# A graph network's propagation written out without loops on TensorE and VectorE, its first operand built by groups, and slot keys computed in two parts

## The reference

```python
def _L0_gnn_ref(x, edge_index):
    K = 16
    ALPHA = 0.1
    ...
    deg = jax.ops.segment_sum(jnp.ones_like(col, dtype=x.dtype), col, num_segments=N)
    deg_inv_sqrt = jnp.where(deg > 0, jax.lax.rsqrt(jnp.maximum(deg, 1e-30)), 0.0)
    norm = (deg_inv_sqrt[row] * deg_inv_sqrt[col])[:, None]
    h = x
    for _ in range(K):
        h_neighbors = jax.ops.segment_sum(norm * h[row], col, num_segments=N)
        h = (1.0 - ALPHA) * h_neighbors + ALPHA * x
    return h
...
x = _layernorm(x + _L0_gnn_ref(x, edge_index), axis=-1)
x = _layernorm(x + _L1_gnn_ref(x, L1_gnn_W0, ..., src, dst), axis=-1)
x = _layernorm(x + _L2_gnn_ref(x, edge_index, edge_weight), axis=-1)
x = _layernorm(x + _L3_gnn_ref(x, edge_index, edge_attr_32, ...), axis=-1)
```

## Time and profile before

| | us |
|---|---|
| runs (three) | 2672.07, 2674.3, 2676.32 |
| median | 2674.3 |
| span of the profiled execution, first to last instruction | 2462.7 |
| median less span | 211.6 |
| PE busy in the span | 2054.2 |
| DVE busy | 1627.3 |
| POOL busy | 1245.4 |

### The profile page before, as it was taken

How to read it: one execution, slowest core, us unless ns; L and a number is a source line. 1 busy time by engine, 2 the same in 40 slices (tenths; PEclk the granted TensorE clock), 3 DMA queues, 4 the chain that set the end, 5 groups by cost and what they waited for, 6 DMA issues and landing times. The chain is left out here.

```text
span 2462.7 us, 56144 instructions
## 1 busy us (share of the span) xinstructions
PE 2054.2 (83%) x21375; PEld 1842.5 (75%) x21375; DVE 1627.3 (66%) x4661; ACT 874.7 (36%) x1203; POOL 1245.4 (51%) x973
## 2 busy tenths in 40 slices
PE   5294539999999999999978859969999969999972
PEld 4142229999999999999977724459989958899872
DVE  6897996555555555555745640077888857888877
ACT  0195530000000000000012100049999918999950
POOL 0380018777778777774000000007777764777763
PEclk9995559999999999999988879969999968999985
DMA  3397002232322223231000059524445423454531
GB/s 135 85 385 266 1 4 22 22 32 22 32 22 22 22 23 32 22 32 22 18 7 2 1 219 355 194 58 125 146 142 165 122 86 101 141 166 127 162 117 40
DMA packets 150939, 227.56 MB, mean 92 GB/s; under 512 B 87649, under 2 KB 109825, under 8 KB 147106
## 3 DMA queue, kind: packets, MB, share of 16 engines
q1 hardware_dynamic: 70994, 186.72, 21.0%
q0 software_dynamic: 74688, 28.51, 11.9%
q10 hardware_dynamic: 5008, 9.07, 1.2%
HBM read 123.37 MB, written 100.84 MB: 91 GB/s over the span
## 5 line engine op out<-in xcount | busy, mean ns | idle before, releaser
L587 PE MATMUL ps<-parts,at 128*128 128x192 f16 x11250 | 960.4, 249 | 52.1 <-DVEq L686 23.5
L587 PEld LDWEIGHTS ps<-parts,at 128*128 128x128 f16 x11250 | 947.0, 99 | 59.8 <-issue 54.3
L1379 POOL DMA_INDIRECT messages_c<-y_table,srci_sb x504 | 509.6, 1011 | 389.3 <-DMA y_table<-ytab 236.4
L628 POOL DMA_INDIRECT weight_matrix<-w,place x392 | 611.9, 1561 | 168.3 <-issue 95.6
L1588 PE MATMUL ps<-yparts,source_onehots_c 128*128 128x192 f16 x7000 | 618.0, 248 | 35.0 <-ACT picked_pairs_c L1419 24.1
L1588 PEld LDWEIGHTS ps<-yparts,source_onehots_c 128*128 128x128 f16 x7000 | 574.2, 98 | 63.0 <-ACT picked_pairs_c L1419 50.3
L707 DVE SCALAR_TENSOR_TENSOR t<-ps,coef,g 128x96 f32<-128x96 f32 x400 | 126.9, 317 | 280.0 <-PE ps L587 278.8
L1407 ACT ACTIVATE source_gaps_c<-sources_spread,unshift 128x1280 f16<-128x1280 f16 x216 | 295.0, 1366 | 19.6 <-ACT source_onehots_c L1410 10.4
L656 ACT ACTIVATE ea_limbs<-ea_in,ea_scale 128x392 f16<-128x392 f32 x32 | 19.9, 621 | 792.5 <-DMA ea_in<-in_eaT 767.3
L1410 ACT ACTIVATE source_onehots_c<-source_gaps_c 128x1280 f16<-128x1280 f16 x216 | 274.4, 1270 | 6.9
L1462 DVE TENSOR_SCALAR source_onehots_c<-sources_spread,shift 128x1280 f16<-128x1280 f16 x484 | 270.4, 568 | 0.4
(11 more groups left out here) (360 smaller groups left out, 1449.7 us busy)
## 6 DMA issues: line engine op xcount, KB each, us to landing
...
edge_limbs<-ea_limbs SPq DMA_DIRECT2D x128, 98.0 KB
...
```

The costliest lines, as they stand in the source:

```text
L587: mm = nc.tensor.matmul(m.ps[:, bank, 0:2 * D], m.at[:, s, blk * P:(blk + 1) * P], parts[:, s, :], start=(s == 0), stop=(s == NB - 1))
L628: nc.gpsimd.indirect_dma_start(cells, bass.IndirectOffsetOnAxis(m.place[:, t:t + 1], 0), m.w[:, t:t + 1], None, compute_op=ALU.add).then_i ...
L1379: nc.gpsimd.indirect_dma_start(msg[:, k % 2, j, :], None, d.yt, bass.IndirectOffsetOnAxis(m.srci[:, k * TURN + j:k * TURN + j + 1], 0)).th ...
```

## The change

In the preparation, the cell addresses move from behind the slot rows into the four waits of DVE for PE. Their place is taken by the reduction of all 12544 attributes at once and a new reduction of x. One `partition_all_reduce` on POOL over both maxima, behind the 14 gathers, replaces the two of before (L487 and L619). The slot keys are computed in two parts of 512 and 384 values, and DVE makes the scale of the propagation (`scale_of` with `m.alls[:, 1:2]`) there. ACT takes over the copy of the second turned table. In the propagation, g0 and its two parts are made in five groups by DVE and ACT in turn, the identity is added on POOL with a semaphore for each block on which PE waits, and the hardware loops of PE and DVE are written out.

The scale of the propagation now comes from the largest |x| rather than from the largest scaled entry. The core of the diff:

```diff
@@ -273,11 +301,16 @@
             nc.gpsimd.iota(jcoli[:], [[P, SG]], 0, 1).then_inc(iotas, 1)
             g.wait_ge(slots, 1)
             for k in range(SG):
+                landed = rows[0] if k < HALVES[0][1] else rows[1]
                 nc.gpsimd.indirect_dma_start(dg[:, k, :], None, d.dst_rows,
-                                             bass.IndirectOffsetOnAxis(ti[:, k:k + 1], 0)).then_inc(rows, 16)
+                                             bass.IndirectOffsetOnAxis(ti[:, k:k + 1], 0)).then_inc(landed, 16)
                 nc.gpsimd.indirect_dma_start(sg[:, k, :], None, d.src_rows,
-                                             bass.IndirectOffsetOnAxis(ti[:, k:k + 1], 0)).then_inc(rows, 16)
-            g.wait_ge(rows, 32 * SG)
+                                             bass.IndirectOffsetOnAxis(ti[:, k:k + 1], 0)).then_inc(landed, 16)
+            g.wait_ge(widest, 1)
+            nc.gpsimd.partition_all_reduce(m.alls[:], m.emax[:], P, RMAX).then_inc(largest, 1)
+            for h, (a, z) in enumerate(HALVES):
+                g.wait_ge(rows[h], 32 * (z - a))
+            g.wait_ge(largest, 1)
...
                 made.then_inc(lows, 1)
+            place_heads(v, do)
             v.wait_ge(free, TN)
             nc.vector.tensor_copy(tally[:], m.ps[0:LOW, 0, 0:HIGH]).then_inc(counted, 1)
+            place_parts(do, 0)
             v.wait_ge(moved, 1)
             do(nc.vector.tensor_copy(m.deg[:], m.ps[:, 1, 0:NB]))
             nc.vector.tensor_scalar(m.dinv[:], m.deg[:], 1.0, None, ALU.add).then_inc(m.var_ready, 1)
             inverse_root(nc, v, do, m, 1, m.dinv[:])
             v.sem_inc(degs, 1)
 
+            place_parts(do, 1)
             v.wait_ge(prefixed, 1)
...
 
+            place_cells(do)
             v.wait_ge(read, 1)
...
 
-            v.wait_ge(srcs, 32)
...
+            v.wait_ge(eal, 16)
+            do(nc.vector.tensor_reduce(m.emax[:, 0:1], eall[:], AX.X, ALU.max, apply_absolute_value=True))
+            v.wait_ge(nodes, 16)
+            do(nc.vector.tensor_reduce(m.emax[:, 1:2], m.x[:].rearrange("p i f -> p (i f)"), AX.X, ALU.max,
+                                       apply_absolute_value=True))
+            v.sem_inc(widest, 1)
...
-            do(nc.vector.tensor_reduce(m.emax[:], emax[:], AX.X, ALU.max))
+            for h, (a, z) in enumerate(HALVES):
+                v.wait_ge(rows[h], 32 * (z - a))
+                own = slice(a, z)
+                do(nc.vector.tensor_copy(rel[:, own, :], dg[:, own, :]))
...
+                do(nc.vector.tensor_scalar(dg[:, own, :], sg[:, own, :], P - 1, None, ALU.bitwise_and))
+                do(nc.vector.tensor_copy(lof[:, own, :], dg[:, own, :]))
+                v.sem_inc(keys, 1)
+            v.wait_ge(largest, 1)
+            scale_of(nc, do, m, m.alls[:, 1:2], m.gs[:], m.gun[:])
             v.wait_ge(turned, 1)
             do(nc.vector.tensor_copy(m.keyT[:], m.ps[:, 4:6, :].rearrange("p a b -> p (a b)")[:, 0:SG * P]))
-            do(nc.vector.tensor_copy(m.lowT[:], m.ps[:, 6:8, :].rearrange("p a b -> p (a b)")[:, 0:SG * P]))
...
             square_root(nc, a, m, 1, m.dinv[:])
+            a.wait_ge(turned, 1)
+            nc.scalar.activation(m.lowT[:], m.ps[:, 6:8, :].rearrange("p a b -> p (a b)")[:, 0:SG * P], ACT.Copy)
...
-            pe.wait_ge(keys, 1)
             for k in range(SG):
+                for h, (first, z) in enumerate(HALVES):
+                    if k == first:
+                        pe.wait_ge(keys, h + 1)
                 nc.tensor.transpose(m.ps[:, 4 + k // 4, (k % 4) * P:(k % 4 + 1) * P], rel[:, k, :], m.ident[:])
                 mm = nc.tensor.transpose(m.ps[:, 6 + k // 4, (k % 4) * P:(k % 4 + 1) * P], lof[:, k, :], m.ident[:])
             mm.then_inc(turned, 1)
...
@@ -484,8 +513,7 @@
         @b.gpsimd
         def _(g):
             nc.gpsimd.memset(m.at[:, :, NW * W:NP], 0.0).then_inc(cleared, 1)
-            nc.gpsimd.partition_all_reduce(m.eall_max[:], m.emax[:], P, RMAX).then_inc(largest, 1)
-            g.wait_ge(largest, 1)
+            g.wait_ge(cleared, 1)
...
         def _(g):
-            g.wait_ge(mx, 1)
-            nc.gpsimd.partition_all_reduce(ga[:], gm[:], P, RMAX).then_inc(amx, 1)
+            for i in range(NB):
+                blk = m.at[:, i, i * P:(i + 1) * P]
+                nc.gpsimd.tensor_tensor(blk, blk, m.ident16[:], ALU.add).then_inc(looped, 1)
...
+            for g in range(NEND):
+                blk = slice(g * ENDS, (g + 1) * ENDS)
+                a.wait_ge(scaled, g + 1)
+                nc.scalar.activation(parts[:, 0, blk, 0:D], g0[:, blk, :], ACT.Copy).then_inc(first, 1)
...
             do = Chain(v, chain)
-            do(nc.vector.tensor_tensor(g0[:], m.x[:], bc_last(m.dinv[:], D), ALU.mult))
-            nc.vector.tensor_reduce(gm[:], g0[:].rearrange("p i f -> p (i f)"), AX.X, ALU.max, apply_absolute_value=True).then_inc(mx, 1)
-
-            for i in range(NB):
-                blk = m.at[:, i, i * P:(i + 1) * P]
-                nc.vector.tensor_tensor(blk, blk, m.ident16[:], ALU.add)
+            do(nc.vector.tensor_scalar(dinvs[:], m.dinv[:], m.gs[:], None, ALU.mult))
+            for g in range(NEND + 1):
+                if g < NEND:
+                    blk = slice(g * ENDS, (g + 1) * ENDS)
+                    nc.vector.tensor_tensor(g0[:, blk, :], m.x[:, blk, :], bc_last(dinvs[:, blk], D),
+                                            ALU.mult).then_inc(scaled, 1)
+                if g >= 1:
+                    blk = slice((g - 1) * ENDS, g * ENDS)
+                    v.wait_ge(first, g)
+                    nc.vector.tensor_tensor(parts[:, 0, blk, D:2 * D], g0[:, blk, :], parts[:, 0, blk, 0:D],
+                                            ALU.subtract).then_inc(ready, ENDS)
             do(nc.vector.tensor_tensor(coef[:], m.dinv[:], m.dinv[:], ALU.mult))
             do(nc.vector.tensor_scalar(coef[:], coef[:], 1.0 - ALPHA, None, ALU.mult))
-            v.wait_ge(amx, 1)
-            scale_of(nc, do, m, ga[:], scl[:], un[:])
-            do(nc.vector.tensor_scalar(g0[:], g0[:], scl[:], None, ALU.mult))
-            do(nc.vector.tensor_copy(parts[:, 0, :, 0:D], g0[:]))
-            do(nc.vector.tensor_tensor(parts[:, 0, :, D:2 * D], g0[:], parts[:, 0, :, 0:D], ALU.subtract))
-            v.sem_inc(ready, NB)
-
-            scale_of(nc, do, m, m.eall_max[:], m.es[:], m.unes[:])
+            v.wait_ge(ready, NB)
+            do(nc.vector.tensor_scalar(g0[:], g0[:], ALPHA, None, ALU.mult))
+
+            scale_of(nc, do, m, m.eall_max, m.es[:], m.unes[:])
             do(nc.vector.tensor_scalar(m.es[:], m.es[:], 2.0 ** -11, None, ALU.mult))
             do(nc.vector.tensor_scalar(m.unes[:], m.unes[:], 2.0 ** 11, None, ALU.mult))
             v.sem_inc(escaled, 1)
-            do(nc.vector.tensor_scalar(g0[:], g0[:], ALPHA, None, ALU.mult))
...
-            with v.Fori(0, STEPS // 2 - 1) as k:
+            for k in range(STEPS // 2 - 1):
                 for r in range(2 * NB):
...
         @b.tensor
         def _(pe):
             pe.sem_inc(taken, NBK)
-            with pe.Fori(0, STEPS // 2) as k:
+            for k in range(STEPS // 2):
                 for r in range(2 * NB):
                     pe.wait_ge(taken, 2 * NB * k + (r + 1))
+                    if k == 0 and r < NB:
+                        pe.wait_ge(looped, r + 1)
 
                     before = (lambda s: pe.wait_ge(ready, 2 * NB * k + (r + s + 1))) if r % NB == 0 else None
                     count_product(nc, m, parts[:, r // NB], r % NB, r % NBK, before).then_inc(prod, 1)
```

85 lines of the change are left out of this document (42 added, 43 removed).

## The result

The changed kernel takes 2614.3 us (median of 4 runs, 2613.4 to 2619.2), the kernel before 2673.2 in the same comparison (4 runs): ratio 0.9785, interval 0.9771 to 0.9799. That is 58.9 us less, where 48.5 were forecast. The time lies 2.7 us under the range's lower end of 2617.

What follows compares the result with a forecast made beforehand. The prediction took PE to bound the propagation, and DVE the preparation and the propagation's start. Its terms, 29.4 + 11.4 + 7.7 = 48.5 us, off 2674.3 gave 2625.8 us, with a range of 2617 to 2644.

Steps and rivals of the forecast that it cites:

- The loops: Propagation: writing out the loops removes PE's gaps between passes and its slow restarts, 29.4 us, at least 18.7.
- rival 2: Propagation: the stalls move into the written-out stream, all 18.7 us of gaps stay, time 2644.5 us; chance 0.08.
- the level in GHz: Propagation: the forecast called PE's granted clock of 0.50 behind the first gap the 1.2 GHz level.
- The start of the propagation: PE starts about 6.4 us behind DVE's first instruction instead of 17.83, saving 11.4 us, bounds 8.6 to 11.8.
- rival 3: Propagation: POOL's additions take over 2.06 us each and pace PE; at 3 us each, 2649 us; chance 0.05.
- The preparation: Its last instruction ends at 100.9 against 108.59, saving 7.7 us, bounds 6.9 to 8.5, given a short all-reduce.
- Rival 1: First all-reduce after a load costs 55 us: both calls, 2731 us, chance 0.04; only the first, 2676, chance 0.03.
- twice the rate: Preparation: of two instruction kinds for 896 values, 0.63 and 1.09 us, the first runs twice as fast; fixed cost 0.17.
- The pause at `largest`: Preparation: if the all-reduce only gets through once DVE stands still at `largest`, it costs 0.8 of the 7.7 us.
- Outside the span: Whole kernel: the 211.6 us between the span of 2462.7 and the median of 2674.3 stay unchanged.
- Rival 4: The longer program costs time outside the span, which would rise by 96 us to give 2722 us; chance 0.04.
- The other stages: Stages besides preparation and propagation keep their work; the count stage loses L487, for which nobody waited, so no gain.

Runs made afterwards that it cites:

- before_unrolled: The kernel before with only the propagation's two hardware loops (PE and DVE) written out; 2428.5 us, ratio 0.9874 to the kernel before.
- after_adds_dve: The changed kernel with the 25 additions of the identity on DVE in place of POOL; 2403.2 us, ratio 0.9754 to the kernel before.
- before_reduce_early: The kernel before with the all-reduce L487 moved from the count stage to the end of the preparation; 2458.4 us, ratio 0.9999 to the kernel before.

## Why the prediction was right and where it was wrong

**The loops** (29.4 us): right in mechanism and size. The trace of before_unrolled gives 29.0 for the stage, the clock stays at 1.00, and no stall went into the straight stream; rival 2 fell. The runs show that the gaps come and go with the loops; what PE waits for behind a back edge no row names. That the gaps go as a whole where the stream is written out was the author's estimate, which no row ahead of it shows; before_unrolled shows 29.0 and a stretch without gaps in its place. The rows give the granted clock as a share of full speed, 0.50 and 1.00; the level in GHz beside it in the forecast is in none of them.

**The start of the propagation** (11.4, bounds 8.6 to 11.8): right in mechanism, a little too large. With the loops' 29.0 taken off the stage's 38.7, 9.7 is left: PE starts 10.4 us earlier, and its matmuls take 827.85 us where they took 827.12 in before_unrolled. POOL's first addition came 6.9 us into the stage, where I had put the end of the load at 5.7, and the 25 took 0.43 each on average for 0.4, so POOL does not pace PE (rival 3). That the first of them meets L719, and takes up to 1.44, was not in the forecast. after_adds_dve shows that PE's start waited for just this strand and not for the parts, of which the last was ready at 347.00 + 0.66 in the changed kernel, 0.8 before PE's start.

**The preparation** (7.7): right, step by step: the keys end at 98.0, the stage at 100.93, the all-reduce takes 0.55 and not 55. Rival 1 fell twice, by this row and by before_reduce_early. The "twice the rate" behind the two-part estimate shows in the durations: DVE's conversions from SBUF take 0.360 us for 384 values (L447) and 0.627 for 896 (L422 before), 0.52 ns a value and 0.16 us fixed, and its copies out of PSUM 0.575 for 400 (L337 before) and 1.091 for 896 (L427), 1.04 ns a value. The pause at `largest`, 0.8, did not come. The all-reduce ran from 92.44 to 92.99, beside L447 and L437, two conversions with one SBUF input each; how it fares beside chained instructions with two is not shown.

**Outside the span**: "the 211.6 us between span and time are carried over" gave the right number for a wrong reason. They were two stages inside the span, 100 us longer each on the chip of the timed runs, as the changed kernel's trace shows and the kernel before's median suggests. Rival 4, built on them, had nothing to stand on: the median less span is 2.0 (2614.3 - 2612.3).

**The step that failed** is "The other stages keep their work. The count stage loses L487, for which nobody waited." This put the count stage at nothing. The work was kept, and the forecast's reason was true, but the clearing's transfers got another source address by the change's new small tiles (packets of 126 ns for 135), and the stage gave 7.2 us. Without them the sum would be 48.5 - 1.7 - 0.4 = 46.4 from the terms as measured; with them 53.6. The missing term alone does not leave the range: 2625.8 - 7.2 = 2618.6. The other 4.3 us down to 2614.3 are a rest of 5.3 and a median of the kernel before that was 1.1 lower this time, less the 2.1 by which two terms were too large. The rest, 58.9 less 53.6, lies behind these stages: `sage` took 3.1 us less in the changed kernel's trace (200.1 and 197.0), but it took from 195.7 to 200.5 in the runs that leave it alone, in the changed kernel with the additions on DVE 200.5 again. The first convolution too, which no edit touches, took from 399.8 to 404.6 off the slow chip. The interval of the first ratio reaches down to 53.7 us. I count nothing of this rest to the change, and it isn't settled.

**The range.** The bounds of the three terms (24 to 29.4, 8.6 to 11.8, 6.9 to 8.5) add up to 39.5 to 49.7 us, thus 2624.6 to 2634.8. That the range began at 2617 rested on no term.
